# Rotary embedding in a cross-attention kernel: the sine products move from VectorE to ScalarE and GpSimd

## What is computed

```python
q = (layernorm(x) @ Wq)          # 32 heads of 128
k = (ctx @ Wk)                   # 8 heads of 128
v = (ctx @ Wv)
rotate_half(u) = concatenate([-u[..., 64:], u[..., :64]])
q = q * cos + rotate_half(q) * sin
k = k * cos + rotate_half(k) * sin
attn = softmax(where(mask == 0, -1e9, q @ k.T / sqrt(128)))
x = x + (attn @ v) @ Wo
x = x + layernorm(x) @ dequantised(Wf) + bias
```

## Time and profile before

| | us |
|---|---|
| median of 3 runs | 1240.17 |
| lowest, highest | 1239.32, 1240.32 |
| profiled execution, its own time | 1243.1 |
| its span in the trace | 1240.9 |
| TensorE, VectorE busy | 1157.4, 1032.9 |
| ScalarE, GpSimd busy | 653.5, 503.4 |
| mean granted TensorE clock | 0.981 |

### The profile page before, as it was taken

One profiled execution on the slowest core, in us unless ns is written; L12 is line 12 of the kernel. 1 busy time (PEld: TensorE's weight loads), 2 busy tenths in 40 slices (PEclk: granted clock), 3 DMA queues, 4 the chain that ended last, 5 costly groups with the idle time before them and its releaser, 6 DMA issues.

```text
span 1240.9 us, 19680 instructions
## 1 busy us (share of the span) xinstructions
PE 1157.4 (93%) x6308; PEld 983.0 (79%) x6320; DVE 1032.9 (83%) x2003; ACT 653.5 (53%) x2169; POOL 503.4 (41%) x394
## 2 busy tenths in 40 slices
PE   3799989999999999997988999999999999999987
PEld 2578878887888878886777788888888888888864
DVE  5878999899989999878888887787777877777786
ACT  3255545555555555645453545555555655555561
POOL 5353443335342443445543434433353434342322
PEclk7999999999999999998998999999999999999999
DMA  5220111112111021112312223111021112110003
GB/s 171 77 77 23 52 43 43 48 31 60 39 41 42 27 68 40 51 45 89 108 54 74 77 86 93 45 35 35 26 60 36 43 27 60 30 48 18 26 26 102
DMA packets 41476, 67.41 MB, mean 54 GB/s; under 512 B 8992, under 2 KB 11168, under 8 KB 41376
## 3 DMA queue, kind: packets, MB, share of 16 engines
q1 hardware_dynamic: 40608, 64.05, 17.6%
q0 software_dynamic: 768, 2.10, 0.5%
HBM read 61.94 MB, written 4.19 MB: 53 GB/s over the span
## 4 chain that ended last, share of the span: by engine, by line
PE 66%; DVE 19%; ACT 4%; issue 4%; DMA 4%; POOL 2%; SPq 0%; ACTq 0%; DVEq 0%; POOLq 0%
PE proj L379 11%; PE proj L380 11%; PE proj L381 10%; PE pO L379 6%; PE pS L468 6%; PE pO L380 6%; PE pO L381 6%; DVE t L728 2%; DVE t L729 2%; PE pV L495 2%; DMA raw<-wo 2%; PE pV L496 2%; PE pT L478 2%; ACT sm L641 2%; PE pO L512 1%
## 5 line engine op out<-in xcount | busy, mean ns | idle before, releaser
L952 POOL TENSOR_TENSOR qT<-qT,t 128x512 f32<-128x512 f32 x128 | 187.3, 1463 | 393.3 <-DVE t L729 393.2
L619 ACT ACTIVATE sm<-pS 128x256 f32<-128x256 f32 x128 | 49.3, 385 | 313.7 <-PE pS L468 313.5
L641 ACT ACTIVATE sm<-sm,tiny 128x64 f32<-128x64 f32 x512 | 172.0, 337 | 77.0 <-DVE tiny L847 75.2
L379 PE MATMUL proj<-XH,QH 128*128 128x512 f32 x512 | 204.8, 400 | 6.1 <-DVE VS L899 4.1
L380 PE MATMUL proj<-XL,QH 128*128 128x512 f32 x512 | 202.6, 396 | 0.0
L381 PE MATMUL proj<-XH,QL 128*128 128x512 f32 x512 | 202.6, 396 | 0.0
L379 PE MATMUL pO<-OH,AH 128*128 128x512 f32 x448 | 181.1, 404 | 12.1 <-DVE acc L815 12.0
L380 PE MATMUL pO<-OL,AH 128*128 128x512 f32 x448 | 176.6, 394 | 0.0
L381 PE MATMUL pO<-OH,AL 128*128 128x512 f32 x448 | 175.9, 393 | 0.0
L468 PEld LDWEIGHTS pS<-kT,qT 128*128 128x128 f32 x1024 | 134.7, 192 | 13.2 <-issue 3.1
L724 DVE TENSOR_TENSOR qT<-proj,COS 128x512 f32<-128x512 f32 x128 | 88.0, 687 | 68.0 <-PE proj L381 40.2
(11 more groups left out here) (129 smaller groups left out, 2565.2 us busy)
## 6 DMA issues: line engine op xcount, KB each, us to landing
raw<-wq SPq DMA_DIRECT2D x64, 256.0 KB
raw<-wo SPq DMA_DIRECT2D x64, 256.0 KB
acc<-x SPq DMA_DIRECT2D x16, 256.0 KB, 3.0
raw<-wk SPq DMA_DIRECT2D x16, 256.0 KB
raw<-ctxT SPq DMA_DIRECT2D x16, 256.0 KB
raw<-wv SPq DMA_DIRECT2D x16, 256.0 KB
rawm<-fbias SPq DMA_DIRECT2D x16, 256.0 KB, 2.8
out<-acc SPq DMA_DIRECT2D x16, 256.0 KB, 2.0
```

The lines of the kernel that those rows point to most:

```text
L379: pe.matmul(dst, lh, rh, start=k == 0, stop=False)
L641: made = act.activation(v4[:, a], v4[:, a], ACT.Exp, bias=nmx[:, a:a + 1], accum_out=rsum[:, a:a + 1])
L952: pool.tensor_tensor(dst, dst, t2[:, :].rearrange("p (a t) -> p a t", t=64), ALU.add).then_inc(made, 1)
```

## The change

VectorE keeps the cosine product only (`times_cos`). ScalarE copies the two halves of the PSUM tile into t2, exchanged (`exchange`): 64 to 127 onto 0 to 63 and the reverse. GpSimd multiplies t2 by SIN in place (`times_sin`) and adds it as before. The sign of the sine table is turned, since the factor is now read at the partition of the output. The bank of q or k is released by ScalarE (a_qx, a_kx). ScalarE's exchange waits for the cosine product (v_qc, v_kc) and for t2 (g_qr, g_kr); for k it waits for the add of q of the same step. GpSimd's product waits for the exchange, its add for the product and the cosine product.

```diff
@@ freed
-            return {"x": (v_xl, i + 1), "q": (v_qs, i + 1), "k": (v_ks, i + 1), "v": (v_vl, i + 1),
-                    "f": (v_fl, i + 1), "m": (v_fa, i + 1), "w": (a_w4, i + 1)}[kind]
+            return {"x": v_xl, "q": a_qx, "k": a_kx, "v": v_vl, "f": v_fl, "m": v_fa, "w": a_w4}[kind], i + 1
@@ scalar: rope
-                    act.wait_ge(v_qs, 4 * (s - 2) + 4)
-                    act.wait_ge(v_ks, s - 1)
+                    act.wait_ge(g_qs, 4 * (s - 2) + 4)
+                    act.wait_ge(g_ks, s - 1)
+            def exchange(b, made):
+                act.copy(t2[0:64, :], proj[64:128, b, :])
+                act.copy(t2[64:128, :], proj[0:64, b, :]).then_inc(made, 1)
@@ scalar: after the scaling of the scores
+                if 0 <= n < PAIRS:
+                    act.wait_ge(v_qc, n + 1)
+                    if n:
+                        act.wait_ge(g_qr, n)
+                    else:
+                        act.wait_ge(e_ct, 4)
+                    if n >= 2 and (n - 1) % 4 == 1:
+                        act.wait_ge(g_kr, (n - 1) // 4 + 1)
+                    exchange(BANK["q", n], a_qx)
@@ scalar: after the casts of weights and the rope tables
+                if 0 <= n < PAIRS and n % 4 == 1:
+                    s = n // 4
+                    act.wait_ge(v_kc, s + 1)
+                    act.wait_ge(g_qr, n + 1)
+                    exchange(BANK["k", s], a_kx)
@@ vector: rotate becomes times_cos
-                dve.tensor_tensor(dst, src.rearrange("p (a t) -> p a t", t=64),
-                                  COS[:, c].rearrange("p (a t) -> p a t", t=64), ALU.mult).then_inc(c_made, 1)
-                if t2_freed:
-                    dve.wait_ge(*t2_freed)
-                dve.tensor_tensor(t2[0:64, :], src[64:128], SIN[64:128, c], ALU.mult)
-                dve.tensor_tensor(t2[64:128, :], src[0:64], SIN[0:64, c], ALU.mult).then_inc(s_made, 1)
+                return dve.tensor_tensor(dst, proj[:, b, :].rearrange("p (a t) -> p a t", t=64),
+                                         COS[:, c].rearrange("p (a t) -> p a t", t=64), ALU.mult)
@@ gpsimd
+            def times_sin(j0, exchanged, count, made):
+                pool.wait_ge(exchanged, count)
+                pool.tensor_tensor(t2[:, :], t2[:, :], SIN[:, 512 * j0:512 * j0 + 512], ALU.mult).then_inc(made, 1)
@@ gpsimd: for q, and the same for k
-                    add_turned(qT[:, n // 4 % 2, :, n % 4, :], v_qc, v_qs, n + 1, g_qr)
+                    s, h = n // 4, n % 4
+                    if h == 0 and s % 16 < 2:
+                        pool.wait_ge(a_cs, 2 * tiles(s)[3] + 2)
+                    times_sin(s % 2, a_qx, n + 1, g_qs)
+                    add_turned(qT[:, s % 2, :, h, :], g_qs, v_qc, n + 1, g_qr)
@@ rope_table
-    return np.ascontiguousarray(np.concatenate([c, c, s, -s], axis=1).astype(np.float32))
+    return np.ascontiguousarray(np.concatenate([c, c, -s, s], axis=1).astype(np.float32))
```

More of the change, by code:

```diff
@@ L200, in build @@
                                               sem("a_w4"))
+        a_qx, a_kx = sem("a_qx"), sem("a_kx")
         v_const, v_idx, v_stat, v_xn, v_fn = sem("v_const"), sem("v_idx"), sem("v_stat"), sem("v_xn"), sem("v_fn")
-        v_lo, v_xl, v_qc, v_qs, v_kc, v_ks = sem("v_lo"), sem("v_xl"), sem("v_qc"), sem("v_qs"), sem("v_kc"), sem("v_ks")
+        v_lo, v_xl, v_qc, v_kc = sem("v_lo"), sem("v_xl"), sem("v_qc"), sem("v_kc")
         v_sm, v_mx, v_ri, v_pn, v_pl, v_al = sem("v_sm"), sem("v_mx"), sem("v_ri"), sem("v_pn"), sem("v_pl"), sem("v_al")
         v_vl, v_ac, v_mk, v_fl, v_fa, v_q = sem("v_vl"), sem("v_ac"), sem("v_mk"), sem("v_fl"), sem("v_fa"), sem("v_q")
-        g_lo, g_qr, g_kr, g_rs, g_fb = sem("g_lo"), sem("g_qr"), sem("g_kr"), sem("g_rs"), sem("g_fb")
+        g_lo, g_rs, g_fb = sem("g_lo"), sem("g_rs"), sem("g_fb")
+        g_qs, g_ks, g_qr, g_kr = sem("g_qs"), sem("g_ks"), sem("g_qr"), sem("g_kr")
         def freed(use):
             kind, i = use
-            return {"x": (v_xl, i + 1), "q": (v_qs, i + 1), "k": (v_ks, i + 1), "v": (v_vl, i + 1),
-                    "f": (v_fl, i + 1), "m": (v_fa, i + 1), "w": (a_w4, i + 1)}[kind]
+            return {"x": v_xl, "q": a_qx, "k": a_kx, "v": v_vl, "f": v_fl, "m": v_fa, "w": a_w4}[kind], i + 1
         def lo_made(i):
@@ L719, in ffn_add, with times_cos @@
                                   ALU.add).then_inc(v_fa, 1)
[L721 removed]
+            def times_cos(b, dst, j0):
                 c = slice(512 * j0, 512 * j0 + 512)
[L723 to L729 removed]
+                return dve.tensor_tensor(dst, proj[:, b, :].rearrange("p (a t) -> p a t", t=64),
+                                         COS[:, c].rearrange("p (a t) -> p a t", t=64), ALU.mult)
             A, B = (F[:, 512 * i:512 * i + 512].bitcast(F32) for i in range(2))
@@ L831, in _ @@
                         dve.wait_ge(e_ct, 8)
-                    k_first = n >= 2 and (n - 1) % 4 == 1
-                    t2_freed = (g_kr, (n - 1) // 4 + 1) if k_first else (g_qr, n) if n else (e_ct, 4)
-                    rotate(BANK["q", n], qT[:, s % 2, :, h, :], s % 2, v_qc, v_qs, t2_freed)
+                    times_cos(BANK["q", n], qT[:, s % 2, :, h, :], s % 2).then_inc(v_qc, 1)
                 if 0 <= m < PAIRS:
@@ L890, in _ @@
                         dve.wait_ge(e_qk, 4 * (s - 2) + 4)
-                    rotate(BANK["k", s], kT[:, s % 2, :].rearrange("p (a t) -> p a t", t=64), s % 2, v_kc, v_ks,
-                           (g_qr, n + 1))
+                    times_cos(BANK["k", s], kT[:, s % 2, :].rearrange("p (a t) -> p a t", t=64),
+                              s % 2).then_inc(v_kc, 1)
                 if v_tile(n):
@@ L980, in _ @@
                     s = n // 4
-                    add_turned(kT[:, s % 2, :].rearrange("p (a t) -> p a t", t=64), v_kc, v_ks, s + 1, g_kr)
+                    times_sin(s % 2, a_kx, s + 1, g_ks)
+                    add_turned(kT[:, s % 2, :].rearrange("p (a t) -> p a t", t=64), g_ks, v_kc, s + 1, g_kr)
 def rope_table():
```

6 lines of the change are left out of this document (2 added, 4 removed).

## The result

The changed kernel takes **1307.39 us** in the median (1303.84 to 1311.06), 1.0541 times the kernel before [1.0522, 1.056]. The direction was forecast, the size was not: +67 us instead of +32, outside the range of 1250 to 1300.

A forecast was written before the change was run, and what follows sets the result against it. VectorE was taken to bound the early steps and TensorE the late ones. Early +32, start +3, middle -8 and late +5 gave +32 us on 1240, so 1272 us, range 1250 to 1300.

The forecast's parts named there:

- the early loss: Steps 9 to 58: closed loop through ScalarE and VectorE, +0.81 us a step without k; +32 us for the stretch.
- I cost it at nothing: GpSimd's 160 added products, 208 us busy, end well before scores need q; no cost except t2's release.
- 1.02 us: ScalarE's pair of exchange copies in each step's loop: what follows starts 1.02 us later, bounds 0.73 and 1.2.
- rival (C): Longer loop: exchange 1.2, no absorption of lag, boundaries at their bound; +25 us more, 1297; chance 0.17.
- -6 for the lag: Early stretch: the 6.8 us in which VectorE waits for TensorE take up some lag, -6 us.
- 0.6 us for that: Six early steps with k and no V: next exchange waits for GpSimd to release t2, 0.6 us each.
- Steps with k: Early: seven with V tiles +1.22 us each (tail +0.41, loop +0.81), +8.5 in all; six without V, 0.
- (D): GpSimd's new products hold up one VectorE operation in each of 50 early steps: +45 us more, 1317; chance 0.08.
- the middle, -8 forecast: Steps 59 to 75: earlier normalisation of x slightly outweighs the loop's cost, half a microsecond in 16 steps, -8 us.
- The bound that I gave (+6): Middle's upper bound: GpSimd's bias add stands behind a product and an add, 0.4 us a step, +6.
- Late, +5 forecast: TensorE stays the bound; group boundaries lose 1.4 us at three without V, 0.3 at three with V: +5.
- Start, +3 forecast: Steps 5 to 8 already run the loop, 4 x 0.8 = +3 us; before them 0, ScalarE having no scores.

The follow-up runs named there:

- the copies alone: Kernel before plus only ScalarE's two 64x512 copies, out of SBUF into an idle tile, in steps 8 to 55 and 80 to 127: 1294.14 us, 1.0429.
- half the exchange: Changed kernel with each of ScalarE's two exchange copies cut to 256 of 512 columns: 1272.71 us, 1.0263.

## Why the prediction was right and wrong

**Right: the mechanism of the early loss, and the sign.** The step rested on the order of ScalarE's queue: the exchange waits for the cosine product, and P, AV and the exponentials stand behind it. Step 28 after the change shows each link, 4.16 us from the first copy of P to the tail exactly as in the earlier trace rows, and the copies alone cost 47 us early.

**Failed: "I cost it at nothing", of GpSimd.** The product and the add were charged only the wait for t2. Without the product 20 of the 67 us go, which is more than half of the 35 us by which the forecast was short. In the profiled executions these are 4 us at the start, 11 early, 5.5 in the middle, 3 late and 1 at the end (24.8 in all; the medians differ by 20). Part of them is the wait for t2, part the quantiser beside the pair, and in the middle the wait for the tables and halves below; how much each is, no run separates. So these us overlap with the items that follow.

**Mis-sized: the exchange.** I took 1.02 us, by the starts of two casts of whole tiles. The two copies start 0.60 apart and the next instruction 0.60 behind: 1.20 us, the bound that I had given to rival (C). PSUM is not the reason: the copies alone read SBUF, and theirs start 0.63 apart at 0.62. The pair to look at stood in the earlier trace rows: ScalarE's two copies of P, one on each half of the partitions, took 0.76 us together, twice the 0.37 of one. The 0.18 a step is 9 us in 50 steps. With it the forecast is 0.99 a step; the median of the fixed part rose by 0.97 (5.79 to 6.76).

**The "-6 for the lag" came, and the wait for t2 took it back.** VectorE's idle time before q's cosine product was 6.8 us in the 50 steps and is 0.1. In the 37 steps without k, what the fixed parts have above their median is 16.3 us in all before and 14.6 after; with a buffer of its own for k it is 8.6. So 7.7 us went, and 6.0 came back in the steps behind a k, whose exchange waits for t2. I had 0.6 us for that in each of six steps. ScalarE waits there longer than I worked out, because product and add took 1.53 and 1.46 us and not 1.30 in the step shown above:

```profile
308.01 1.53 POOL L965 TENSOR_TENSOR t<-t,SIN 128x512 f32<-128x512 f32 x1 [0.68 <-ACT t L611]
...
307.52 0.89 DVE L788 SCALAR_TENSOR_TENSOR F<-F 128x256 f32<-128x256 f32 x2
...
309.52 0.44 DVE L857 COPY_PREDICATED sm<-mk,tiny 128x256 f32<-128x256 uint8 x1
310.00 0.42 DVE L861 TENSOR_REDUCE tiny<-sm 128x4 f32<-128x256 f32 x1
```

Both GpSimd instructions (the add starts at 309.62) started while VectorE was at work on tiles in SBUF: the second of the two L788, and L857.

**Steps with k.** With V tiles they grew by 1.40 us each instead of 1.22 (9.8 us, not 8.5), though before the change some of them waited for TensorE, and that wait is gone. The tail alone rose by 0.97 where I had 0.41:

```profile
267.65 0.68 DVE L744 TENSOR_TENSOR kT<-proj,COS 128x512 f32<-128x512 f32 x1
270.35 0.86 DVE L913 TENSOR_TENSOR VS<-proj,VS 64x256 fp32r<-64x256 f32 x2 [2.02 <-ACT VS L678]
271.25 1.04 DVE L790 TENSOR_SCALAR tiny<-tiny 128x8 f32<-128x8 f32 x1
...
270.97 1.29 POOL L970 TENSOR_TENSOR kT<-kT,t 128x512 f32<-128x512 f32 x1
```

V's low halves start 2.70 us after k's cosine product, not 2.55, and behind them an operation on eight elements takes 1.04 us beside GpSimd's add: (D) at one place. Without V they changed by -0.3 each, near the 0 that I took, but the wait for t2 is charged to the step behind it.

Together, early: 9 for the exchange, 2.4 for t2 (6.0 less 3.6), 2.7 for the tails with V tiles (7 x 0.38), less 1.7 of lag: 12.4 us of the 12.6 that were missing. Nothing is left over that the lower clock would have to explain.

**Wrong sign: the middle, -8 forecast, +8.4 measured.** The normalised x did come sooner. TensorE's waits in this stretch (total us, times, longest), before and then after:

```profile
PE proj L393 <- DVE rawx L696: 10.3, 5, 3.4
...
PE pS L468 <- ACT SIN L604: 2.7, 1, 2.7
PE proj L379 <- DVE VS L899: 2.2, 1, 2.2
...
PE proj L379 <- DVE XL L707: 0.8, 1, 0.8
```
```profile
PE pS L471 <- ACT SIN L607: 7.1, 2, 5.6
PE proj L382 <- DVE XL L728: 6.4, 2, 3.7
PE proj L382 <- DVE VS L913: 5.1, 5, 2.8
...
PE proj L396 <- DVE rawx L717: 2.4, 3, 1.4
```

The wait for the normalised x shrank by 7.9 us. Three others took its place, +4.4, +5.6 and +2.9: for the rope tables, for x's low part and for V's low halves. All three begin with work of ScalarE (the copies from PSUM, the high parts), which now stands behind an exchange. I costed what VectorE does sooner and not what ScalarE does later. With the rest of the list the waits add up to 4.6 us more than before. The other 3.8 us are TensorE's own busy time, 179.5 us instead of 175.7, at a mean granted clock of 0.93 instead of 0.94; why, no run shows. Around step 62 the chain also runs through a DMA; ScalarE and TensorE:

```profile
633.86 0.62 ACT L581 CAST CH<-raw 128x512 fp32r<-128x512 f32 x1 [3.50 <-DMA raw<-ctxT]
...
634.96 1.94 PE L471 MATMUL pS<-kT,qT 128*128 128x64 f32 x8 [5.56 <-ACT SIN L607]
```

The rope tables stand behind a cast that waits 3.50 us for its DMA, and by the kernel's waits the DMA starts when GpSimd has made the low part of an earlier weight, whose cast stands behind an exchange. That step takes 15.0 us instead of 12.8. With half the exchange the three waits are 6.2, 3.4 and 3.9 us and the stretch is 6.7 shorter; without GpSimd's product 6.2, 3.7 and 4.5, and 5.5 shorter. The two overlap, so how much is ScalarE's and how much GpSimd's part stays open. The bound that I gave (+6) had only the bias add as its cause.

**Late, +5 forecast, +7.0 measured.** The mechanism holds. TensorE at the fourth output weight's cast answers to the earlier trace rows:

```profile
973.65 0.50 PE L515 MATMUL pO<-OH,AH 128*128 128x512 f32 x1 [1.27 <-ACT OH L581]
```

The wait grew by 0.71 us, and the boundaries without V cost 2.0 us each instead of 1.4; those with V 0 to 0.5 (0.3 taken). **Start, +3 forecast, +6.7:** the same omission. TensorE's waits for the rope tables ahead of step 9 are 5.4 us where they were 0.5; I had written that ScalarE has no scores to serve there, and it has the tables. Without GpSimd's product 4 us of it go.

**Rival (D)** got 0.08, since the pair would stand beside reads of PSUM. For q it does, and VectorE's work in SBUF is hardly hit there. VectorE's 104 operations on the quantiser's tile F in the early stretch took 59.0 us before and 60.5 after the change; 84.5 with the exchange behind the casts, and 60.7 with the product taken out there.

So at the size that I gave it (+45) it didn't come true in the change itself; what there is of it stands behind k, where the pair meets the quantiser. It is what stops the repairs: with the exchange behind the casts, and again with the pair a step later, the pair came beside VectorE's work in SBUF.

**The sum of the misses:** early 12.6, middle 16.4, start 3.7, late 2.0, end 1.6, together 36 us of the span. The medians differ by 67.2, the spans by 68.4. The range failed because it took the unknowns one by one: (C) had the longer loop, at 1297, but no case added GpSimd's product or a loss in the middle to it.

## What to carry to other kernels

Before work is moved to an engine that is half idle, write down what stands behind it in that engine's queue and who waits for that: an engine's idle time is worth nothing if the new work waits for the engine that it relieves. Add up the closed loop through both engines, and follow the casts that free a buffer to the DMA that waits for it. Charge every engine that the work moves to, also the one that seems far from full. A cheap test is to add the new work alone and leave the old in place, and its counterpart is to take one part of the new work out: together they told that the copies cost 47 us early, the relief was worth about 13 and GpSimd's product took 11 of these.

## What the runs showed of the hardware

- ScalarE's pairs of copies on the two halves of the partitions don't overlap: 64x512 from PSUM take 0.58 us and start 0.60 apart, from SBUF 0.62 and 0.63 apart, 64x256 from PSUM 0.37 and 0.38 apart. Instructions on all 128 partitions behind each other do, by 0.1 us, out of SBUF (casts of 128x512: 0.61 us, 0.51 apart) and out of PSUM (the two copies of a rope table, 128x128: 0.26 us, 0.16 apart).
- VectorE's elementwise instructions that touch SBUF alone (products, scalar forms with one input, the predicated copy) and start beside a two-input GpSimd instruction of 128x512 last until that one has ended and then nearly their own time: 8 elements a partition take up to 1.04 to 1.22 us for 0.17, a 128x256 product 1.31 for 0.42, the low part of a weight (128x512) 1.77 for 0.69. Every such case in these traces is hit, down to 8 elements a partition; instructions on one element keep their 0.15 us (28 cases).
- Not hit are VectorE's instructions that read PSUM (0.69 beside the product) and, from SBUF too, its reductions (0.42 for 128x256 in 878 cases, as at 310.00 above), reciprocals (0.18 in 156) and the statistics of the layer norm (0.68).
- The other way round GpSimd's instruction is the longer one: 1.53 and 1.46 us for 1.30, when it starts during such a VectorE instruction.
- Two GpSimd instructions of which the second needs the first start 1.37 us apart at 1.30 us each; two low parts behind each other start 1.24 apart.
- Reading a PSUM bank by ScalarE and VectorE at once, cosine product and exchange in parallel, was not tried; all versions keep one behind the other. It is the repair left untested.
